# Counting products of two graph-attention passes in the float32r kind, with a larger dense share and the gather ring moved

## What is computed

```python
h = x @ W                                   # 3125 x 128
alpha = leaky_relu((h @ att_s)[src] + (h @ att_d)[dst] + edge_term)
ex = exp(alpha - segment_max(alpha, dst)[dst])
w = ex / segment_sum(ex, dst)[dst]
out = segment_sum(w[:, None] * h[src], dst) + b
```

## Time and profile before

| what | value |
|---|---|
| median of three runs | 1996.36 us |
| span of the profiled execution | 1993.2 us, mean granted TensorE clock 0.910 |
| first attention pass | from 1044.6 to 1311.9 us of the span |
| second attention pass | from 1421.5 to 1688.5 us of the span |

### The profile page before, as it was taken

One profiled execution on the slowest core, in us unless ns is written; L12 is line 12 of the kernel. 1 busy time (PEld: TensorE's weight loads), 2 busy tenths in 40 slices (PEclk: granted clock), 3 DMA queues, 4 the chain that ended last, 5 costly groups with the idle time before them and its releaser, 6 DMA issues. The chain is left out here.

```text
span 1993.2 us, 43518 instructions
## 1 busy us (share of the span) xinstructions
PE 1706.9 (86%) x13678; PEld 1412.5 (71%) x13678; DVE 1396.3 (70%) x4290; ACT 913.6 (46%) x2490; POOL 982.6 (49%) x1002
## 2 busy tenths in 40 slices
PE   6799999999999749998649998956599989399996
PEld 5699999999998715556547886756478768166664
DVE  5677888888887698996667765556777654745556
ACT  2566676776776366773305553420255433411100
POOL 3766677777776120000557777735677774300000
PEclk9799999999999759999659999976699999699998
DMA  6887788888877002332532111117121111345442
GB/s 193 252 249 239 231 252 243 249 252 255 254 240 230 10 5 84 128 123 112 174 91 66 43 43 42 49 61 185 43 66 42 41 44 37 121 176 202 175 166 89
DMA packets 149677, 276.91 MB, mean 139 GB/s; under 512 B 28807, under 2 KB 88845, under 8 KB 147188
## 3 DMA queue, kind: packets, MB, share of 16 engines
q1 hardware_dynamic: 109134, 191.58, 29.5%
q0 software_dynamic: 35456, 79.88, 14.3%
q10 hardware_dynamic: 4854, 2.55, 0.5%
HBM read 228.82 MB, written 45.08 MB: 137 GB/s over the span
## 5 line engine op out<-in xcount | busy, mean ns | idle before, releaser
L972 POOL DMA_INDIRECT gated_rows<-p_tab,src_idx x416 | 429.0, 1031 | 176.4 <-issue 102.2
L1364 POOL DMA_INDIRECT ring<-table,src_idx x384 | 382.9, 997 | 145.3 <-issue 89.3
L2194 PE MATMUL bank<-counts,mean_xs 128*128 128x416 bf16 (+2 forms) x1350 | 220.1, 322 | 32.1 <-DVE mean_xs L1696 32.1
L1013 PE MATMUL bank<-gated_wide_q,gated_comb 128*128 128x256 f32 x832 | 218.6, 386 | 0.0
L1170 DVE TENSOR_TENSOR gated_pre<-bank,gated_rows 128x512 f32<-128x512 f32 x208 | 142.8, 687 | 105.1 <-PE bank L1013 103.0
L1496 ACT COPY attention_counts<-bank 128x475 f32 (+1 forms) x224 | 127.6, 570 | 183.7 <-PE bank L1523 179.9
L2194 PEld LDWEIGHTS bank<-counts,mean_xs 128*128 128x128 bf16 x1350 | 126.3, 98 | 116.6 <-issue 35.1
L1086 ACT ACTIVATE gated_sig<-gated_pre 128x512 f32<-128x512 f32 x208 | 131.2, 631 | 155.3 <-DVE gated_pre L1170 153.3
L1534 PE MATMUL bank<-attention_counts,h_sb 128*128 128x232 f32 (+1 forms) x900 | 193.3, 342 | 0.5 <-issue 0.5
L1534 PEld LDWEIGHTS bank<-attention_counts,h_sb 128*128 128x128 f32 x900 | 159.2, 192 | 28.3 <-issue 1.5
L1519 PE MATMUL bank<-attention_wide_a,scratch 128*128 128x300 f32 x448 | 161.1, 442 | 12.2 <-DVE scratch L1577 11.2
(11 more groups left out here) (440 smaller groups left out, 3985.9 us busy)
## 6 DMA issues: line engine op xcount, KB each, us to landing
counts<-count_tabs SPq DMA_DIRECT2D x16, 2675.0 KB, 9.9
h_sb<-in_edge_attr_dram SPq DMA_DIRECT2D x51, 512.0 KB, 4.9
count_tabs<-mean_counts SPq DMA_DIRECT2D x40, 535.0 KB, 2.7
gated_relr<-rel_rows SPq DMA_DIRECT2D x104, 128.0 KB
gated_ids<-id_rows SPq DMA_DIRECT2D x26, 512.0 KB
gated_wide_q<-q_tab SPq DMA_DIRECT2D x208, 64.0 KB
attend_hot_lo<-low_hots SPq DMA_DIRECT2D x52, 256.0 KB
gated_ea<-in_edge_attr_dram SPq DMA_DIRECT2D x51, 256.0 KB
```

Of the source, the lines that this page charges most:

```text
L972: pool.indirect_dma_start(out=rows[:, q % TICKS, c, :], out_offset=None, in_=p_tab, in_offset=bass.IndirectOffsetOnAxis(ap=src_idx[:, b, j ...
L1013: mm = pe.matmul(PRE[q % 2][:, c * 2 * P:(c + 1) * 2 * P], comb[:, u, k, c, :], wide_q[:, u, c, :], start=True, stop=True)
L1364: pool.indirect_dma_start(out=rows[:, n % RING, j, :], out_offset=None, in_=table, in_offset=bass.IndirectOffsetOnAxis(ap=src_idx[:, gathe ...
L2194: mm = pe.matmul(BANKS_D[q % ND][:, 0:width], xs[l][:, m // 3, m % 3, :], counts[:, s % 2, m // 3, at:at + width], start=(m == 0), stop=(m ...
```

## The change

- The count products take operands of the kind float32r instead of float32. The weight moves from `wide` into `lo`, in two parts: `w_c`, which is rounded to that kind as it is written into `lo`, and `w_left`, what is missing to the full float32 weight. Each chunk now has two products, with `lo` of either part, against the same `wide`, which holds zeros and ones: four products of 300 columns in a step instead of two.
- DVE makes `lo` with four operations on 128 columns (comparison and multiplication, two per-partition scalars), and `wide` with two operations on 300 columns that only compare (one per-partition scalar), written as float32r. `src_lo` becomes a float32 tensor; the mean layers' `lo` reads it too.
- `second_at` is rounded down to an even number, by two small operations on DVE and two on POOL in the prologue.
- AT_DENSE is 8: 128 count steps and 40 gathered batches in a pass. Applied blocks are 260 columns wide (132 for the last two) and take 16 steps.
- The ring of gathered rows is no tensor of its own: six of its batches lie in `cur`, two in the upper part of `y_sb`.
- At the end of the attend stage there are four operations where there were two: `w_high` (rounded weights), `w_c`, `w_left`, `w_tab`.

```diff
+F32R = mybir.dt.float32r
...
-NSB, AT_DENSE = 8, 7
+NSB, AT_DENSE = 8, 8
...
+TO_EVEN = 1.5 * 2.0 ** 24
...
-    src_lo = sb("src_lo", [P, NB, J], BF16)
+    src_lo = sb("src_lo", [P, NB, J])
...
-    A_BLOCKS = cut_blocks([ATP] * LEAP + [ATP // 2] * 2, [232] * LEAP + [120] * 2, [0] * (LEAP + 1) + [120])
+    A_BLOCKS = cut_blocks([ATP] * LEAP + [ATP // 2] * 2, [260] * LEAP + [132] * 2, [0] * (LEAP + 1) + [132])
...
-    w_tab, w_c = sb("w_tab", [P, NB, J]), sb("w_c", [P, NB, J])
+    w_tab, w_c, w_left = sb("w_tab", [P, NB, J]), sb("w_c", [P, NB, J]), sb("w_left", [P, NB, J])
...
+                    counted("apart2", dve.tensor_scalar(froms[:, 1:J:2], froms[:, 1:J:2], -0.5, TO_EVEN, ALU.add, ALU.add))
+                    after_("apart2")
+                    counted("apart3", dve.tensor_scalar(froms[:, 1:J:2], froms[:, 1:J:2], -TO_EVEN, None, ALU.add))
+                    after_("apart3")
...
+                    link(pool.tensor_scalar(second_f[:, :], second_f[:, :], -0.5, TO_EVEN, ALU.add, ALU.add))
+                    link(pool.tensor_scalar(second_f[:, :], second_f[:, :], -TO_EVEN, None, ALU.add))
...
+    RING_A = NT * P // (J * P)
...
+    def ring_row(n, j):
+
+        at, slot = (cur, n % RING) if n % RING < RING_A else (y_sb, n % RING - RING_A + J)
+        return flat_of(at)[:, (slot * J + j) * P:(slot * J + j + 1) * P]
...
+    def gather_row(pool, table, rows_in, n, j):
+
+        pool.indirect_dma_start(out=ring_row(n, j), out_offset=None, in_=table,
                                 in_offset=bass.IndirectOffsetOnAxis(ap=src_idx[:, gathered_batch(n), j:j + 1], axis=0)
...
-            lo_at = HB * J * W
-            row_at = lo_at + LR * 2 * P
-            lo = scratch[:, lo_at:row_at].rearrange("p (r c n) -> p r c n", r=LR, c=2)
+            row_at = HB * J * W
+            lo = sb("lo", [P, LR, 2, 2, P], F32R)
...
-            wide_a, wide_b = sb("wide_a", [P, WR, NT * WA]), sb("wide_b", [P, WR, NT * WA])
+            wide_a, wide_b = sb("wide_a", [P, WR, NT * WA], F32R), sb("wide_b", [P, WR, NT * WA], F32R)
...
-                        pe.matmul(to[:, :, 0:WA], lo[:, n % LR, 0, :], wide_a[:, n % WR, :], start=True, stop=False, skip_group_check=True)
+                        for part in range(2):
+                            pe.matmul(to[:, :, 0:WA], lo[:, n % LR, 0, part, :], wide_a[:, n % WR, :], start=(part == 0), stop=False, skip_group_check=True)
                         if closes(A_BLOCKS, n):
                             pe.wait_ge(nothing, 2)
                             pe.matmul(to[:, :, WA:WP], lo_iota[:, :], blank[:, :], start=False, stop=False, skip_group_check=True)
-                        pe.matmul(to[:, :, bass.ds(at, WA)], lo[:, n % LR, 1, :], wide_b[:, n % WR, :], start=False, stop=True,
-                                  skip_group_check=True).then_inc(counted, 1)
+                        for part in range(2):
+                            mm = pe.matmul(to[:, :, bass.ds(at, WA)], lo[:, n % LR, 1, part, :], wide_b[:, n % WR, :], start=False, stop=(part == 1),
+                                           skip_group_check=True)
+                        mm.then_inc(counted, 1)
...
                         first, size, width, at = A_BLOCKS[k]
...
-                            mm = pe.matmul(BANKS_G[n % 2][:, 0:W], rows[:, n % RING, j, :], hot[:, n % HB, j, :],
+                            mm = pe.matmul(BANKS_G[n % 2][:, 0:W], ring_row(n, j), hot[:, n % HB, j, :],
...
                     def make_lo(n):
                         b, k = dense(n)
                         reach(dve, counted, n - LR + 1)
-                        dve.tensor_tensor(lo[:, n % LR, :, :], lo_iota[:, :].rearrange("p (a n) -> p a n", a=1).broadcast_to([P, 2, P]),
-                                          src_lo[:, b, 2 * k:2 * k + 2].rearrange("p (j n) -> p j n", n=1).broadcast_to([P, 2, P]),
-                                          ALU.is_equal).then_inc(lo_ready, 1)
+                        for c in range(2):
+                            j = 2 * k + c
+                            for part, w in enumerate((w_c, w_left)):
+                                ins = dve.tensor_scalar(lo[:, n % LR, c, part, :], lo_iota[:, :], src_lo[:, b, j:j + 1], w[:, b, j:j + 1],
+                                                        ALU.is_equal, ALU.mult)
+                        ins.then_inc(lo_ready, 1)
 
                     def make_wide(n):
                         b, k = dense(n)
                         reach(dve, counted, n - WR + 1)
-                        dve.tensor_scalar(wide_a[:, n % WR, :], code_iota[:, 0:NT * WA], code[:, b, 2 * k:2 * k + 1], w_c[:, b, 2 * k:2 * k + 1],
-                                          ALU.is_equal, ALU.mult)
-                        dve.tensor_scalar(wide_b[:, n % WR, :], code_iota[:, :], code[:, b, 2 * k + 1:2 * k + 2], w_c[:, b, 2 * k + 1:2 * k + 2],
-                                          ALU.is_equal, ALU.mult).then_inc(wide_ready, 1)
+                        dve.tensor_scalar(wide_a[:, n % WR, :], code_iota[:, :], code[:, b, 2 * k:2 * k + 1], None, ALU.is_equal)
+                        dve.tensor_scalar(wide_b[:, n % WR, :], code_iota[:, :], code[:, b, 2 * k + 1:2 * k + 2], None, ALU.is_equal).then_inc(wide_ready, 1)
...
+            found, w_high = sb("found", [P, NB * J]), sb("w_high", [P, NB, J], F32R)
...
-                    for n, to in enumerate((w_c, w_tab)):
-                        dve.wait_ge(t, 10 + n)
-                        dve.tensor_copy(to[:, :, :], bank[n][:, 0:NB * J].rearrange("p (j b) -> p b j", b=NB)).then_inc(spare, 1)
+                    by_chunk, by_row = [bank[n][:, 0:NB * J].rearrange("p (j b) -> p b j", b=NB) for n in range(2)]
+                    dve.wait_ge(t, 10)
+                    link(dve.tensor_copy(w_high[:, :, :], by_chunk))
+                    dve.tensor_copy(w_c[:, :, :], by_chunk).then_inc(spare, 1)
+                    dve.tensor_tensor(w_left[:, :, :], by_chunk, w_high[:, :, :], ALU.subtract).then_inc(spare, 1)
+                    dve.wait_ge(t, 11)
+                    dve.tensor_copy(w_tab[:, :, :], by_row).then_inc(spare, 1)
...
-        with nc.sbuf_tensor(f"ring{l}", [P, RING, J, P], F32) as rows:
-            rows_in = [kept_sem(f"rows{l}_in{i}") for i in range(RING)]
-            attend(l, x_sb if l == 1 else cur, tables[l], rows, rows_in, a_s, a_d)
-            attention_pass(l, tables[l], rows, rows_in)
+        rows_in = [kept_sem(f"rows{l}_in{i}") for i in range(RING)]
+        attend(l, x_sb if l == 1 else cur, tables[l], rows_in, a_s, a_d)
+        attention_pass(l, tables[l], rows_in)
```

More of the change, by code:

```diff
@@ L1360, in gathered_batch, with attention_pass @@
         return n // AG * SB_BATCHES + AT_DENSE + n % AG
-    def gather_row(pool, table, rows, rows_in, n, j):
-        pool.indirect_dma_start(out=rows[:, n % RING, j, :], out_offset=None, in_=table,
+    RING_A = NT * P // (J * P)
+    def ring_row(n, j):
+        at, slot = (cur, n % RING) if n % RING < RING_A else (y_sb, n % RING - RING_A + J)
+        return flat_of(at)[:, (slot * J + j) * P:(slot * J + j + 1) * P]
+    assert (RING - RING_A + J) * J * P <= NT * P and J * BE <= J * J * P
+    def gather_row(pool, table, rows_in, n, j):
+        pool.indirect_dma_start(out=ring_row(n, j), out_offset=None, in_=table,
                                 in_offset=bass.IndirectOffsetOnAxis(ap=src_idx[:, gathered_batch(n), j:j + 1], axis=0)
                                 ).then_inc(rows_in[n % RING], 16)
-    def attention_pass(l, table, rows, rows_in):
+    def attention_pass(l, table, rows_in):
         with phase(f"attention{l}") as (sb, sem):
@@ L1434, in attention_pass @@
             only_when, fall_sp, fall_pool, fall_pe, fall_dve = edge_pass(
-                f"attention{l}", sb, sem, table, rows[:, 0:LB * PAIRS, :, :].rearrange("p r j d -> p (r j d)"), scratch[:, 0:HB * J * W], finished, weights=w_tab)
+                f"attention{l}", sb, sem, table, flat_of(cur)[:, 0:UN * J * P], scratch[:, 0:HB * J * W], finished, weights=w_tab)
             with nc.Block() as block:
@@ L1452, in _ @@
                             reach(pool, counted, (J * (n - RING + 2) + j) * NDW // (J * NGB))
-                            gather_row(pool, table, rows, rows_in, n, j)
+                            gather_row(pool, table, rows_in, n, j)
                         if n == AUX_FROM:
@@ L2319, in aux_nodes, with attend @@
         return bank[7][:, 0:NT * k].rearrange("p (t k) -> p t k", k=k)
-    def attend(l, x_from, table, rows, rows_in, a_s, a_d):
+    def attend(l, x_from, table, rows_in, a_s, a_d):
         H = P + 2
```

1 line of the change is left out of this document (removed).

## The result

The changed kernel takes 2002.3 us (median of five runs, 1999.78 to 2006.13) against 1994.45 for the kernel before beside it on the same chip: a ratio of 1.0035, 95% interval 1.002 to 1.005. The forecast was 2003, slower by a third of a per cent. The profiled execution has a span of 2001.8 us at a mean clock of 0.896.

The account below looks back on a forecast made before the run. TensorE was taken to set the pace, GpSimd close behind; after the change VectorE. Two passes +3.8, attend +2.6, prologue +0.4 make +6.8: span 1993.2 becomes 2000, plus 3.2 gives 2003 us; range 1970 to 2045, likeliest case 1988 to 2020.

Parts of the forecast that it names:

- What bounds the kernel before: In the two passes: TensorE's 235.7 us and POOL's 250 both lie under 267 and together make it, TensorE setting the pace.
- GpSimd's price at eight batches: Gathers in a pass: 161 at 1.30 us with the pause make 209 of 269 us, leaving slack of 60.
- TensorE's price: Products in a pass: 0.127 us per float32r product, 0.44 per 260 columns; sum 189.0 us, 46.7 less.
- VectorE's work: DVE in a pass: `lo` four at 0.257, `wide` two at 0.289, `join` 0.11, a step 1.72 instead of 1.14; sum 247.
- the rival by 0.067 fixed: DVE's operations: fixed part only 0.067, `lo` 0.134 and `wide` 0.223 each, TensorE bounds, pass 212, time 1890; chance 0.02.
- the one by one column a cycle: DVE's float32r writes: each column costs 1.04 ns, +0.58 a step, 74 a pass, time 2151; chance 0.07.
- Loads, waits, the end: DVE in a pass: 6 us for register loads, 8 of waits, 7.8 from the last `wide` to the last add.
- the first rival: DVE's loads and waits vanish in its full queue: pass 252.6, time 1970 to 1992; chance 0.30.
- The serial rival: Gathered step: register read, one-hot, weighings, copy and join hold DVE, 17 us a pass more, time 2037; chance 0.15.
- Edits at nothing: `src_lo` in float32, even offsets and the ring in `cur` and `y_sb`: 0 us each.
- Attend: End of the attend stage: two copies at 0.6 to 0.69 become four operations of the same size, +1.3 in each layer.
- The clock: TensorE's clock may be granted less with gaps, half speed making 189 us 378; in the sum at 0.

Follow-up runs that it names:

- my first expectation: For the changed kernel with seven of thirteen batches by counts again: passes of 252 to 264 us, time 1968 to 1991; measured 2012.6 us, ratio 1.0105.
- The runs with 35 us more or less: Changed kernel with two more float32r products a step, left side zeros: 2012.1 us, ratio 1.0102; without TensorE's `w_left` products: 1998.6 us, ratio 1.0018.
- the first run: Kernel before with only the ring in `cur` and `y_sb`, `src_lo` in float32 and the even offsets: ratio 0.9992.
- share alone, old kind: Kernel before with the small edits, eight batches by counts and blocks of 260 and 132 columns, old float32 products kept: ratio 0.9994.
- three by ScalarE: Changed kernel with VectorE making a plain one-hot and ScalarE three of the four `lo` left sides: 1959.4 us, ratio 0.9811.
- three by ScalarE, old share: Changed kernel with ScalarE making three of four left sides, but seven batches by counts and blocks of 232 and 120 columns: 1994.0 us, ratio 1.0009.
- two by ScalarE: Changed kernel with VectorE making a plain one-hot and two left sides, ScalarE the two low ones: 1974.5 us, ratio 0.990.
- VectorE's part left out: Changed kernel with VectorE making only the two high left sides a step, TensorE running all four products with `w_c`: 1930.8 us, ratio 0.9686.
- kind alone, old share: Changed kernel with seven of thirteen batches by counts again and blocks of 232 and 120 columns: 2012.6 us, ratio 1.0105.
- without scalars: Changed kernel with `lo` made by three `tensor_tensor` operations of 256 columns instead of four two-scalar ones: 2019.6 us, ratio 1.0115.

## Why the prediction came out right, step by step

- **What bounds the kernel before**: half right. I wrote that TensorE sets the pace and POOL is close behind, and that both lie under 267. GpSimd's 250 us lacked what must follow its last gather. With the 12 to 16 us that the traces show there, it makes 262 to 266 by itself. Nothing hung on it at eight batches, where 33 us lie behind GpSimd's last gather, some 20 more than must follow it; at seven it would have been a wrong forecast, and my first expectation was one.
- **GpSimd's price at eight batches**: wrong, and hidden. The prediction kept 1.30 for a gather with its pause and had 209 of 269 us. A gather with its pause takes 1.41, the waits for free places in the ring add 10 us, and the last one starts at 236. Of the slack of 60 us that the prediction counted on, 33 were left.
- **TensorE's price**: the kind does what it says. The term was 0.127 a product and a product takes 0.138, a step 0.55 instead of 0.51. With that, and the prediction's other terms (260 columns measure 0.438, as put in), TensorE has 71 + 88 + 36 = 195 us, not 189. After a stop the first product takes 0.215, a step then 0.63. The runs with 35 us more or less show why the 6 us cost nothing.
- **VectorE's work**: the term that decides, right. `lo` was put at 0.257 and is 0.256 in the median (0.260 in the mean), `wide` at 0.289 and is 0.285 in the median, joins at 0.11 and are 0.107, the gathered step at 0.473 and is 0.46. The sum was 247; the profile has DVE busy 249. The value of `wide`, built from the price of one scalar, was the one without a row of its own; the rival by 0.067 fixed and the one by one column a cycle fall with it. The rule of the Trainium skill ("VectorE: DVE Perf Modes", The TRN2 errata) would have `lo` at 0.13, and the trace has 0.256; the same section says that the rule comes out too low for a single operation.
- **Loads, waits, the end**: 6 + 8 + 7.8 = 22 were put in, and 269.7 - 248.9 = 21 measured, in other parts: 6.9 for the loads, as said; 4.4 for the block adds' registers, which I had among the work; 3.5 in waits for ACT and at gathered steps, not 8; 5.2 for the last block. The waits and the end were put 7 us too high, and the loads, the registers and the work (247 for 249) some 7 too low. That the sum met 269 within 1 us is luck to that extent. Of the first rival (loads and waits vanish) 4.5 us of waits came true; the loads stayed and the block adds' part grew, so it falls.
- **The gathered step**: covered, as said. DVE waited for ACT three times, 1.4 us in all. The serial rival falls.
- **Edits at nothing**: none that shows, by the first run. Attend: +0.9 in each layer, not +1.3, since the four operations start 0.5 to 0.6 us apart, not 0.6 to 0.69. The prologue's 0.4 is too small for any run here to show.
- **The clock**: in the sum at full speed. It fell from 0.98 to 0.92 in the passes. The second pass by parts:

```profile
1425.80:1470.00 44.20, 34.46 (x128) 29.92 (x128) 41.67 (x160) 18.29 (x44) 27.78 (x24) 0.50 0.21 55
1470.00:1688.00 218.00, 186.86 (x1112) 158.35 (x1112) 206.28 (x822) 102.11 (x252) 149.96 (x137) 1.00 0.15 36
```

  So TensorE has half the clock for the first 44 us and the full one from there on; in the kernel before the half clock lasts for the first 6 us and returns twice for 3 to 4. It cost nothing that shows: in those 44 us DVE is busy 41.7 and never waits for TensorE. The prediction had not reckoned with so long a stretch; DVE being the bound hid it.
- **The sum**: 2 x 2.5 + 2 x 0.9 + 0.4 (the last as put in) = 7.2, against 6.8 put in and 7.85 between the medians. The likeliest case's own range was 1988 to 2020, so a hit within 1 us is closer than its terms allowed for.

## What to carry over

Price the engine that receives the work as closely as the one that is freed: here some 41 us less work on TensorE turned on 0.69 us more of VectorE's work in each of 128 steps. A queue's bound ends with what must follow its last item, not with that item. And when one part of a change costs two engines something, take it off each engine alone: two runs then say whose work the time is made of. Taken off both at once, the time here met the number of the wrong engine.

## What the runs showed of the hardware

- **VectorE's work slows GpSimd's gathers.** From the changed kernel's 1.104 us, taking products off TensorE leaves 1.109, and taking `lo` operations off VectorE gives 1.057. The mean of a gather in the second pass, by what VectorE does beside it (its two-scalar operations of 128 columns, and its busy share):

| kernel | `lo` operations with two scalars | VectorE busy | mean of a gather, us |
|---|---|---|---|
| share alone, old kind | 0 | 0.70 | 1.009 |
| three by ScalarE | 128 | 0.81 | 1.003 |
| three by ScalarE, old share | 112 | 0.70 | 0.998 |
| two by ScalarE | 256 | 0.89 | 1.052 |
| VectorE's part left out | 256 | 0.80 | 1.057 |
| kind alone, old share | 448 | 0.82 | 1.064 |
| without scalars | 0 | 0.91 | 1.042 |
| changed kernel | 512 | 0.92 | 1.104 |

  It rises roughly with both columns (the first three rows are one level). Two scalars by themselves are not the cause: the first row's kernel has 256 `wide` operations with two scalars and 300 columns in a pass. Without such operations 1.042 are left at a busy share of 0.91; whether by the operations on two tensors or by the share no run parts. The shortest gathers in all traces take 0.94. The Trainium skill ("GPSIMD Engine Reference", Specifications) says that GpSimd's way into SBUF is shared with VectorE and contended by instructions in a two-port mode or with two SBUF inputs. The runs agree that VectorE's work slows the gathers; which of its instructions are in such a mode, and which one hits which gather, the trace doesn't tell.
- **TensorE's granted clock in a pass comes in stretches of the half and the full level.** With VectorE's work the same, the half clock takes 64 us of the second pass with 35 us of TensorE's work left out, 44 in the changed kernel and 24 with 35 us more (means 0.88, 0.92, 0.96). In all three the pass begins at the half clock. TensorE's busy time alone doesn't order the passes: 228 us of 269.7 go with 0.92, and 230 of 277.9, with its stops for rows, with 0.88.
- **The first product after a stop of TensorE takes some 0.08 us longer**: a float32r one 0.215 instead of 0.138, a float32 record of 260 columns 0.295 instead of 0.219 (seven in the changed kernel's second pass). A step of float32r products between float32 ones costs 0.55, four times 0.138, so mixed kinds have no price of their own here.
